# Normalised rows turned by DMA transposes in two halves, six latents behind the last projection

## The reference

```python
x = x + attention(layernorm(x))          # eps 1e-5
x = x + ffn(layernorm(x))
# attention: q = rmsnorm(x @ wq_a.T) @ wq_b.T (16 heads, latent of 384); kv latent of 128 and a rotary key of 64
#            softmax(q k^T / sqrt(192)) v, then @ wo.T
# ffn:       (silu(x @ gate_w * gate_scale) * (x @ up_w * up_scale)) @ down_w * down_scale   (1536 wide)
```

## Time and profile before

| | us |
|---|---|
| median of 3 runs (lowest, highest) | 2204.91 (2204.39, 2205.18) |
| the profiled execution | 2204.99 |
| its span | 2203.2 |
| PE busy | 2178.1 (99%) |
| DVE, POOL, ACT busy | 1590.6 (72%), 1361.7 (62%), 1282.7 (58%) |
| granted TensorE clock | 1.000 of full |

### The profile page before, as it was taken

How to read it: one execution, slowest core, us unless ns; L and a number is a source line. 1 busy time by engine, 2 the same in 40 slices (tenths; PEclk the granted TensorE clock), 3 DMA queues, 4 the chain that set the end, 5 groups by cost and what they waited for, 6 DMA issues and landing times.

```text
span 2203.2 us, 37444 instructions
## 1 busy us (share of the span) xinstructions
PE 2178.1 (99%) x11728; PEld 1100.2 (50%) x11728; DVE 1590.6 (72%) x3577; ACT 1282.7 (58%) x2698; POOL 1361.7 (62%) x1083
## 2 busy tenths in 40 slices
PE   7999999999999999999999999999999999999999
PEld 5444544445445564455644555445554556445554
DVE  8888886877577775777767777577766777467773
ACT  6666564554377732876328763387444874357732
POOL 4657465785388733987249772498535884368742
PEclk9999999999999999999999999999999999999999
DMA  7867436665168930788318882188723896148830
GB/s 249 189 124 153 93 72 155 151 141 128 29 127 161 172 91 19 154 162 166 78 32 158 164 155 65 42 169 158 144 59 61 168 168 130 25 92 164 151 83 20
DMA packets 734362, 265.44 MB, mean 120 GB/s; under 512 B 687312, under 2 KB 703696, under 8 KB 733136
## 3 DMA queue, kind: packets, MB, share of 16 engines
q1 hardware_dynamic: 734160, 263.05, 58.0%
HBM read 79.31 MB, written 14.81 MB: 43 GB/s over the span
## 4 chain that ended last, share of the span: by engine, by line
PE 92%; DVE 3%; ACT 1%; POOL 1%; DMA 1%; issue 1%; SPq 1%; DVEq 0%; POOLq 0%; ACTq 0%
PE bank L1130 13%; PE bank L943 9%; PE bank L356 7%; PE bank L358 7%; PE bank L357 7%; PE scores L1140 7%; PE scores L358 5%; PE scores L357 5%; PE scores L356 5%; PE scores L829 5%; PE bank L848 4%; PE bank L849 4%; PE bank L850 4%; PE scores L826 3%; PE bank L1117 1%; PE scores L721 1%
## 5 line engine op out<-in xcount | busy, mean ns | idle before, releaser
L1826 DVE TENSOR_REDUCE mx<-scores 128x1 f32<-128x512 f32 x512 | 353.0, 689 | 61.3 <-PE scores L358 60.9
L2359 POOL TENSOR_TENSOR arena<-arena 128x1024 f16<-128x1024 f32 x168 | 354.4, 2131 | 37.4 <-ACT arena L1387 37.4
L1371 ACT ACTIVATE arena<-scores,shift 128x512 f32<-128x512 f32 x336 | 229.4, 686 | 147.0 <-DVE shift L1828 102.0
L1130 PE MATMUL bank<-arena,WFF 128*128 128x512 f16 x1392 | 313.5, 379 | 0.8 <-DVE arena L2150 0.6
L1911 DVE SCALAR_TENSOR_TENSOR arena<-bank,arena 128x512 f32<-128x512 f32 x336 | 217.0, 686 | 76.2 <-PE bank L943 74.8
L2460 POOL TENSOR_TENSOR arena<-arena 128x512 f16<-128x512 f32 x96 | 115.1, 1199 | 247.3 <-ACT arena L1540 247.3
L2272 POOL TENSOR_TENSOR arena<-arena 128x1024 f16<-128x1024 f32 x88 | 188.1, 2141 | 94.1 <-ACT arena L1361 93.7
L1130 PEld LDWEIGHTS bank<-arena,WFF 128*128 128x128 f16 x1392 | 135.9, 98 | 164.1 <-DVE arena L2150 2.3
L943 PE MATMUL bank<-WVO 128*128 128x256 f16 x1764 | 213.5, 273 | 0.3 <-DVE arena L1911 0.3
L829 PE MATMUL scores<-arena 128*128 128x512 f16 x512 | 195.4, 382 | 0.0
L943 PEld LDWEIGHTS bank<-WVO 128*128 128x128 f16 x1764 | 172.1, 98 | 46.1 <-DVE arena L1911 1.3
(11 more groups left out here) (204 smaller groups left out, 4694.2 us busy)
## 6 DMA issues: line engine op xcount, KB each, us to landing
WVO<-w_duo SPq DMA_DIRECT2D x42, 512.0 KB, 4.4
WVO<-w_duo SPq DMA_DIRECT2D x42, 384.0 KB, 3.9
arena<-arena SPq DMA_TRANSPOSE x712, 3.3
arena<-w_ffn SPq DMA_DIRECT2D x24, 384.0 KB, 3.5
arena<-x SPq DMA_DIRECT2D x8, 1024.0 KB, 5.7
out<-arena SPq DMA_DIRECT2D x32, 256.0 KB, 2.0
arena<-x SPq DMA_DIRECT2D x14, 512.0 KB, 4.5
WVO<-w_o SPq DMA_DIRECT2D x4, 1024.0 KB, 8.1
```

Source lines behind the costliest of these rows:

```text
L1130: m = pe.matmul(dst[:, :], lhsT=w[:, c, k, :], rhs=XT[:, p, k, :], start=(k == 0 and p == 0), stop=(k == NK - 1 and p == 1))
L1826: dve.tensor_reduce(mx[:, t:t + 1], SC[:, t, :], AX_X, ALU.max).then_inc(s["mxr"], 1)
L2359: pool.tensor_tensor(PL[:, par, two, :], exps(i)[:, two, :], PH[:, par, two, :], ALU.subtract).then_inc(s["pl"], 1)
```

## The change

The rows of batches 1 to 6 are turned by four DMA transposes (`turn_rows`: high and low half of tiles 0 and 1, then of tiles 2 and 3) instead of PE's 16. ACT rounds `XN2` itself to the high half `XHL` (`x_rows_hi`), DVE takes the low half (`x_rows_lo`), and the feed-forward reads `XTT`. PE makes the gates of chunks 0 and 1 by halves, as the transposes land (`turned_gates`). The latent k1 moves behind the last projection, also in batch 0, and k3 follows q3. The sums of the rows come out of `add_out`, the sums of squares from ACT (`squares`, before used in batch 7 alone), also in batch 0; DVE works out the root for two tiles at a time, with the first low halves placed between the steps of the second root. In batches 2 to 6 ACT takes the high half of the last context. Batch 0 keeps its transposes on PE; batch 7 is left as it was.

```diff
@@ -80,7 +80,7 @@
 
-LATENTS = [("q", 0), ("k", 0), ("k", 1), ("q", 1), ("q", 2), ("k", 2), ("q", 3), ("k", 3)]
+LATENTS = [("q", 0), ("k", 0), ("q", 1), ("q", 2), ("k", 1), ("k", 2), ("q", 3), ("k", 3)]
 N_CT = NH + 1
@@ -218,6 +218,8 @@
         XT = carve(o_xt, F16, 2, NK, S)
+        XTT = carve(o_xt, F16, 2, NT, NK, P)
+        XHL = carve(o_pbuf + 8192, F16, 2, NT, H)
         XR = carve(o_xr, F32, NT, H)
@@ -271,8 +273,8 @@
         SETUP_KBANK = (BQ, BT, BC, BO)
-        KBANK = (SC[:, 0], SC[:, 1], SC[:, 3], BO)
-        QBANK = (BQ, BQ, SC[:, 2], BT)
+        KBANK = (SC[:, 0], SC[:, 1], SC[:, 3], SC[:, 1])
+        QBANK = (BQ, BQ, SC[:, 2], SC[:, 0])
         VBANK_LAST = (BQ, BC)
@@ -357,9 +360,12 @@
-        def latent_banks(setup):
+        def latent_banks(setup, a=None):
...
-            return {"q": q, "k": list(SETUP_KBANK) if setup else list(KBANK)}
+            k = list(SETUP_KBANK) if setup else list(KBANK)
+            if isinstance(a, int) and a == 1:
+                q[3], k[3] = BT, BO
+            return {"q": q, "k": k}
@@ -531,6 +537,15 @@
                                        STG[:, p, two, :].rearrange("p t h -> p (t h)")).then_inc(s["xt1"], 16)
+
+            def turn_rows(b, half):
+
+                two = slice(2 * half, 2 * half + 2)
+                for p, made in enumerate(("xth", "xtl")):
+                    sp.wait_ge(s[made], (b + 1) * NT + 2 * half + 2)
+                    sp.sem_inc(s["turn"])
+                    sp.dma_start_transpose(XTT[:, p, two].rearrange("p t k q -> p (t k) q"),
+                                           XHL[:, p, two, :].rearrange("p t h -> p (t h)")).then_inc(x_t[p][half], 16)
 
@@ -621,6 +636,9 @@
                 sp.dma_start(DSC, down_scale.rearrange("(a d) -> a d", a=1).broadcast_to((P, H))).then_inc(s["ld_dsc"], 16)
+                if not (first or last):
+                    turn_rows(b, 0)
+                    turn_rows(b, 1)
                 if first:
@@ -1075,8 +1093,6 @@
                 latent("k", 0)
-                pe.wait_ge(s["ph"], ph + 2)
-                latent("k", 1)
                 project_out(b, final, 0)
@@ -1090,11 +1106,19 @@
                 latent("q", 2)
+                latent("k", 1)
                 pe.wait_ge(s["ph"], ph + 4)
-                pe.wait_ge(s["outr"], ph + 4)
+                if b >= B_PLAIN:
+                    pe.wait_ge(s["outr"], ph + 4)
                 latent("k", 2)
-                latent("q", 3)
-
+                if first:
+                    pe.wait_ge(s["outr"], ph + 2)
+                else:
+                    pe.wait_ge(s["lat"], lat + 2)
+                latent("q", 3, a=b + 1)
+                if not first:
+                    pe.wait_ge(s["lat"], lat + 5)
+                    latent("k", 3, a=b + 1)
 
@@ -1103,21 +1127,47 @@
 
+                def rows(p, k, half=None):
+                    if last or first:
+                        return XT[:, p, k, :] if half is None else XT[:, p, k, 2 * half * P:2 * half * P + 2 * P]
+                    return XTT[:, p, :, k, :] if half is None else XTT[:, p, 2 * half:2 * half + 2, k, :]
+
+                def first_pass(half, p, c, names="gu"):
+
+                    rounded(2 * c + 2)
+                    c0, c1 = 2 * half * P, 2 * half * P + 2 * P
+                    for name in names:
+                        w, dst = (WG, GBANK(c)) if name == "g" else (WU, UBANK(c))
+                        for k in range(NK):
+                            m = pe.matmul(dst[:, c0:c1], lhsT=w[:, c, k, :], rhs=rows(p, k, half),
+                                          start=(k == 0 and p == 0), stop=(k == NK - 1 and p == 1))
+                        if half and p:
+                            m.then_inc(s["gu"], 1)
+
                 def first_gates(half, chunks):
 
-                    rounded(2)
-                    c0, c1 = 2 * half * P, 2 * half * P + 2 * P
                     for p, made in enumerate(("xth", "xtl")):
-                        pe.wait_ge(s[made], u * NT + c1 // P)
+                        pe.wait_ge(s[made], u * NT + 2 * half + 2)
                         for c in chunks:
...
                                 pe.wait_ge(s["outr"], B * NH * NT - (2 if c else 0))
-                            for w, dst in ((WG, GBANK(c)), (WU, UBANK(c))):
-                                for k in range(NK):
-                                    m = pe.matmul(dst[:, c0:c1], lhsT=w[:, c, k, :], rhs=XT[:, p, k, c0:c1],
-                                                  start=(k == 0 and p == 0), stop=(k == NK - 1 and p == 1))
-                                if half and p:
-                                    m.then_inc(s["gu"], 1)
+                            first_pass(half, p, c)
+
+                def turned_gates():
+
+                    pe.wait_ge(s["outr"], (b + 1) * (NH * NT))
+                    pe.wait_ge(s["lat"], (b + 1) * (2 * NT) + 3)
+                    for p in range(2):
+                        pe.wait_ge(x_t[p][0], b * 16)
+                        first_pass(0, p, 0)
+                        first_pass(0, p, 1)
+                    pe.wait_ge(x_t[0][1], b * 16)
+                    first_pass(1, 0, 0)
+                    first_pass(1, 0, 1, "g")
+                    pe.wait_ge(x_t[1][1], b * 16)
+                    first_pass(1, 1, 0)
+                    first_pass(1, 0, 1, "u")
+                    first_pass(1, 1, 1)
 
@@ -1174,23 +1224,27 @@
                     first_gates(1, (0, 1))
-                else:
+                elif first:
                     for t in range(NT):
...
                             pe.wait_ge(s["outr"], (b + 1) * (NH * NT))
-                            latent("k", 3)
-                        pe.wait_ge(s["lat"], (b + 1) * (2 * NT) + (2, 3, 5, 6)[t])
+                            latent("k", 3, a=b + 1)
+                        pe.wait_ge(s["lat"], (b + 1) * (2 * NT) + (2, 5, 4, 6)[t])
                         x_transposes(u, t, XN2)
...
                     first_gates(1, (0,))
+                else:
+                    turned_gates()
                 for c in range(1, NF):
-                    if c == 1 and not last:
+                    if c == 1 and first:
                         pe.wait_ge(s["lat"], (b + 1) * (2 * NT) + 2 * NT)
-                    if c > 1 or not last:
+                    if c > 1 or first:
                         gate_up(c)
...
                     elif c >= 2 and not (last and c == NF - 1):
+                        if c == 2 and not (last or first):
+                            pe.wait_ge(s["lat"], (b + 1) * (2 * NT) + 2 * NT)
                         down(c - 2)
@@ -1273,15 +1327,22 @@
                 for t in tiles:
-                    act.wait_ge(s["xtp"], u * NT + t + 1)
+                    act.wait_ge(s["xtp"], (u if u < 2 else 2) * NT + t + 1)
                     act.activation(XT[:, 0, :, tile(t)], SC[:, t, :].rearrange("p (k n) -> p k n", k=NK), ACT.Copy,
...
 
+            def x_rows_hi(b, t):
+
+                if t == 0:
+                    act.wait_ge(s["ctp"], (b + 1) * N_CT)
+                act.wait_ge(s["xn"], (b + 1) * NT + t + 1)
+                act.activation(XHL[:, 0, t, :], XN2[:, t, :], ACT.Copy, scale=XS).then_inc(s["xth"], 1)
+
             def latent(a, i, setup=False):
...
                 n, raw = (QL, QN[:, t, :]) if which == "q" else (KL, KRAW[:, t, :])
-                src = latent_banks(setup)[which][t]
+                src = latent_banks(setup, a)[which][t]
                 act.wait_ge(s["qkv"], a * (2 * NT) + (i + 1))
@@ -1520,12 +1581,29 @@
                     return
-                for i in range(2, 2 * NT - 2):
-                    latent(b + 1, i)
-                x_hi(b + 1, (0, 1))
-                latent(b + 1, 2 * NT - 2)
-                x_hi(b + 1, (2, 3))
-                latent(b + 1, 2 * NT - 1)
+                if not plain:
+                    context_half_hi(b, 0, VBANK_LATE, NH - 1)
+                    context_half_hi(b, 1, VBANK_LATE, NH - 1)
+                for t in range(NT):
+                    squares(b, t, (b * NH + NH - 1) * NT + t + 1)
+                latent(b + 1, 2)
+                if first:
+                    for i in range(3, 2 * NT - 2):
+                        latent(b + 1, i)
+                    x_hi(b + 1, (0, 1))
+                    latent(b + 1, 2 * NT - 2)
+                    x_hi(b + 1, (2, 3))
+                    latent(b + 1, 2 * NT - 1)
+                    return
+                latent(b + 1, 3)
+                x_rows_hi(b, 0)
+                x_rows_hi(b, 1)
+                latent(b + 1, 4)
+                latent(b + 1, 5)
+                x_rows_hi(b, 2)
+                x_rows_hi(b, 3)
+                latent(b + 1, 6)
+                latent(b + 1, 7)
 
@@ -1549,7 +1627,12 @@
                     chunk = ffn_chunk(c) if first else None
-                    tanh(c)
+                    if first or last or c != 1:
+                        tanh(c)
```

(65 more changed lines are left out.)

39 lines of the change are left out of this document (20 added, 19 removed).

## The result

| | before | after |
|---|---|---|
| median of 20 runs each, us | 2204.91 | 2208.20 |
| lowest, highest | 2203.64, 2206.94 | 2206.76, 2209.67 |
| profiled execution | 2204.99 | 2207.44 |
| its span | 2203.2 | 2205.6 |

The account below looks back on a forecast made before the run. PE's work plus its few waits bounds the kernel. Batches 2 to 6 give -0.33 each (-1.65), batch 1 +0.52, batch 0 +0.99, together -0.1: 2204.9 us for the profiled execution, 2204.8 against the median; range 2198.5 to 2209.

Parts of the forecast that it names:

- the landing of the transposes of tiles 2 and 3: Gates of chunk 1: high halves issued at 10.12, PE on at 13.25; low halves issued 11.48, free PE at 14.86.
- its own sign of being wrong: Prediction wrong if rounding starts before q2, landings differ from 3.1 by over half a microsecond, or chunk 2 waits.
- The second rival: Border transposes land late behind the load of `DSC` in SP's queue: +0.92 in six batches, 2210.3 us; chance 0.13.
- Waits at an undisturbed border: Behind the last projection, both chunks' gates issued at 17.04 instead of 15.80: waits of 1.24 us in all.
- P: Start of the first matmul behind the last projection: 0.85 us sooner in batches 2 to 6, unmoved in batches 0 and 1.
- the first wait (0.7): Ahead of the gates: PE waits 0.67 us for the rows of tiles 0 and 1, starting at 9.49.
- the two later ones (0.27, 0.30): Within the gates: PE waits for the high, then the low halves of tiles 2 and 3, 0.27 and 0.30 us.
- Batch 0: Keeps its transposes and gates and has k1 behind the last projection: 0.99 us longer.
- Batch 1: Rows turned by DMA, but the last projection starts no sooner: 0.52 us longer.
- The end without a wait: Border with no wait: gates could start at 8.82 behind the last projection's start, both chunks issued at 15.80.
- ACT bound by q2: ACT must evacuate q2 before rounding tiles 0 and 1, so their high halves start only at 5.09.
- Chunk 2 just in time: DVE's gate step for chunk 0 ends at 16.91, chunk 2 needs its bank at 17.04; uncovered, some 0.1 a batch.

Follow-up runs that it names:

- the stand-in without waits: Changed kernel with plain DMAs for transposes, and ACT rounding tiles 0 and 1 ahead of the fourth latent: 2197.81 us, ratio 0.9966 to the kernel before.
- the stand-in: Changed kernel with each DMA transpose replaced by a plain DMA of the same bytes, nothing turned: 2202.59 us.
- the stand-ins: Copies of the kernels before and after with plain DMAs of the same bytes for DMA transposes: 2202.34 and 2202.59 us; the experiments edit these copies.

## Why the prediction was wrong

**The step that failed** is the landing of the transposes of tiles 2 and 3. The prediction gave every transpose 3.13 to 3.38 us and said of late ones that nothing else is in flight. The code loads were: in three of six batches one falls into the third or fourth transpose, and these took 3.46, 3.89 and 4.92 us (third) and 3.05, 3.65 and 4.35 us (fourth, in batch 3 issued 0.94 late). That is its own sign of being wrong, landings over half a microsecond off. In batches 3, 4 and 5 the price is 0.84 + 0.70 + 1.73 = 3.27 us over what undisturbed batches take. Another load falls near the last probabilities in batch 7. The second rival had the right kind of loss, late landings, but a wrong place (SP's queue) and the same price for all six. The two rows that I took a duration from the earlier trace rows were undisturbed ones.

By the Trainium skill, DMA: Bandwidth & Descriptors, on why a DMA counts its semaphore up by 16, each engine that takes part adds one when its share has landed, so that only the full count says that all has. For the plain copies the trace agrees: most packets run on, and the copy lands with a few late ones. For the transposes it is not the whole of it: there nearly all packets stop, and a load of 0.96 us made the third transpose of batch 5 land 1.7 us late. Why they stop no run here shows.

**The sum of the rest.** Without these loads the borders would be 0.66 - 3.27 = -2.6 us by this count, where the prediction had -0.1: it expected 2.5 us too much there. The profiled execution less the 3.27 is 2204.2, near the 2204.9 forecast for it, but by luck: the 1.8 us outside the borders (below) make up for most of that. At the borders:
- Waits at an undisturbed border: 1.24 forecast; 20.07 against the 19.26 of the stand-in without waits is 0.81. The gates started at P+9.54 to P+9.63 for P+9.49, so the first wait (0.7) was right; the two later ones (0.27, 0.30) hardly came. The third transpose was issued at P+9.88 for 10.12, since ACT was through with tiles 2 and 3 at 9.80 for 10.02; the fourth at 11.23 for 11.48, and it landed after 3.08 for 3.38. This is the largest term: 0.4 a batch.
- P: forecast 0.85 sooner in batches 2 to 6; 1.14 in batch 2, 0.79 in the others. Batches 0 and 1: P unmoved, right, with a wait ahead of head 14's projection of 1.80 and 1.09 us (1.2 to 2.0 forecast).
- Batch 0: +0.99 forecast, +0.99 measured, and confirmed by taking it back. Batch 1: +0.52 forecast, +0.23 measured.
- The end without a wait, P+8.82 and 6.98 for the gates: confirmed when the rows were made sooner (8.82, 19.26).
- ACT bound by q2: right, rounding at P+4.95 for P+5.09. That this bond was itself made by moving k1 behind P, and cost 1.4 us a border, the prediction did not see: it priced the move as 0.99 of PE's time shifted from one side of P to the other.
- Chunk 2 just in time: no wait there.

**Outside the borders** the profiles differ by +1.8 us, which the prediction didn't have. In the last batch 0.98, of which the wait for its last values is 0.74. The other 1.02 is spread over the heads of batches 0 to 5 by -0.23 to +0.47 each; in the stand-ins these stretches agree within 0.25. One wait of it is visible, 0.34 us for transposed probabilities in batch 4 (at 1453.71): a transpose stops from 1450.6 to 1451.3 as above, behind a packet of 8 KB at 1450.0 on a second queue of instruction loads (q14, 127 packets; none falls into the borders of batches 1 to 6). Where the rest comes from was not settled, nor the 0.8 us by which the medians differ more than the two profiled executions.

**What is shown and what argued.** That loads make copies late, and that this costs PE 0.2 to 1.3 us each, is shown by moving them in the stand-in. For transposes no load was moved; that loads make them late rests on the changed kernel's trace: the same places, its three late batches and no others, and packets that stop while a load holds an engine. The stand-in's undisturbed borders are 0.1 us shorter, and its loads cost less, so the gain of 5 us for the rounding ahead of the fourth latent can't be carried over in size.

## What to carry to other kernels

When work moves from the bounding engine to a DMA that it then waits for, count the landing's spread and not its median, and leave slack of a microsecond or start the DMA sooner: what was cover before is now on the path. Ask what the engine that feeds the DMA has in front of it; an order that saves the bounding engine some time can hold up the feeder by more (here 0.8 against 1.4 us). And a difference of a microsecond or two between versions may be only where the code loads fall; compare borders one by one before a cause is named. Where a plain copy stands in for a transpose, look at the packets of both: here a load held back a share of the one and stopped the other.

## What the runs showed of the hardware

- A load of 16 KB of instructions takes one DMA engine for 0.88 to 1.6 us (changed kernel, 90 loads). A 256 KB transpose in flight landed up to 1.7 us later (4.92 for 3.18 us), a 256 KB copy within SBUF up to 1.3 us (4.26 for 2.94).
- While and after a load holds an engine, a copy's other packets go on (922 in 1.1 us around a load) and nearly all of a transpose's stop (25 in 1.1 us): at the three late borders 19 to 24 of them stayed open, the longest for 0.79, 1.14 and 1.56 us, and at no border of the stand-ins a packet for more than 0.35 us.
- Ninety waits that are met at once, at the start of PE's program, moved the loads by 2 to 6 us for the rest of the program, and with them waits of up to 1.4 us; batch 0 began 0.7 and 2.2 us later.
- Copies of 256 KB within SBUF landed 0.1 us later in pieces of 128 bytes than of 256 (3.04 for 2.94, 3.17 for 3.04 us).
- At a border of the stand-in the list of waits showed 0.3 of the 0.7 us lost: 0.17 lay under the last matmul's latency and 0.24 in gaps too short for the list.
